# Attention with an interleaved feed-forward part: key projection ahead of the output products in steps 34 to 61

## The reference

```python
x = x + xattn(layernorm(x), ctx, mask, ...)   # 32 heads of 128, 8 batches of 128 tokens
x = x + ffn(layernorm(x), w_gate, w_up, w_down)

def xattn(h, c, mask, position_bias, ln_weight, w_q, w_k, w_v, w_out):
    x = rmsnorm(h, ln_weight)
    q, k, v = x @ w_q.T, c @ w_k.T, c @ w_v.T          # 512 -> 32 * 128
    score = softmax(where(mask, q @ k.T + position_bias, -inf))
    return h + (score @ v) @ w_out.T

def ffn(x, w_gate, w_up, w_down):                       # 512 -> 1376 -> 512
    h = silu(fq(x) @ fq(w_gate).T) * (fq(x) @ fq(w_up).T)
    return fq(h) @ fq(w_down).T                         # fq: 8 bit fake quantization
```

## Time and profile before

| | us |
|---|---|
| median of 3 runs | 1030.38 (1029.58 to 1031.2) |
| the profiled execution, whole | 1029.58 |
| its span, first to last instruction | 1027.9 |
| PE busy | 1005.1 (98%) |
| DVE busy | 690.2 (67%) |
| ACT busy | 512.8 (50%) |
| GpSimd busy | 457.2 (44%) |

### The profile page before, as it was taken

One profiled execution on the slowest core, in us unless ns is written; L12 is line 12 of the kernel. 1 busy time (PEld: TensorE's weight loads), 2 busy tenths in 40 slices (PEclk: granted clock), 3 DMA queues, 4 the chain that ended last, 5 costly groups with the idle time before them and its releaser, 6 DMA issues.

```text
span 1027.9 us, 18615 instructions
## 1 busy us (share of the span) xinstructions
PE 1005.1 (98%) x6215; PEld 848.8 (83%) x6215; DVE 690.2 (67%) x1833; ACT 512.8 (50%) x1298; POOL 457.2 (44%) x361
## 2 busy tenths in 40 slices
PE   8999999999999999999999999999999999998987
PEld 7888888888888888888888888888888888864465
DVE  6666565656658776868765566558656665768977
ACT  4445444444454454444554355254535635546764
POOL 4554444444443454542444435344443634523441
PEclk9999999999999999999999999999999999999999
DMA  7332233332222333332422123222221222100002
GB/s 266 120 100 90 88 99 99 100 100 81 86 90 89 99 101 102 88 122 95 143 88 88 58 65 88 87 68 75 88 64 58 88 88 77 48 21 23 1 1 83
DMA packets 50414, 87.74 MB, mean 85 GB/s; under 512 B 6368, under 2 KB 15200, under 8 KB 50336
## 3 DMA queue, kind: packets, MB, share of 16 engines
q1 hardware_dynamic: 50336, 86.76, 27.2%
HBM read 84.64 MB, written 2.10 MB: 84 GB/s over the span
## 4 chain that ended last, share of the span: by engine, by line
PE 87%; DVE 7%; DVEq 2%; issue 1%; ACT 1%; DMA 0%; POOL 0%; SPq 0%; ACTq 0%
PE pX L1836 17%; PE pX L1838 16%; PE pX L1837 16%; PE pT L2112 6%; PE oacc L1891 5%; PE pS L2036 5%; PE oacc L1898 5%; PE oacc L1895 5%; PE pS L1841 3%; PE pX L1969 1%; PE pT L2025 1%; PE pX L2025 1%; PE pX L1841 1%; DVE silu L1572 1%; DVE h_s L1575 1%
## 5 line engine op out<-in xcount | busy, mean ns | idle before, releaser
L582 POOL TENSOR_TENSOR wq_lo<-raw_q,wq_hi 128x512 fp32r<-128x512 f32 x64 | 82.7, 1292 | 298.2 <-DVE prob L1448 288.5
L1836 PE MATMUL pX<-wv_lo,cT_hi 128*128 128x256 f32 x512 | 149.2, 291 | 0.2 <-ACT q_sb L769 0.2
L897 ACT ACTIVATE prob<-score,neg_max 128x128 f32<-128x128 f32 x256 | 99.8, 391 | 98.3 <-DVE neg_max L1434 98.3
L1837 PE MATMUL pX<-wv_hi,cT_lo 128*128 128x256 f32 x512 | 144.0, 281 | 0.0
L1838 PE MATMUL pX<-wv_hi,cT_hi 128*128 128x256 f32 x512 | 144.0, 281 | 0.0
L582 POOL TENSOR_TENSOR wv_lo<-raw_v,wv_hi 128x1024 fp32r<-128x1024 f32 x32 | 77.1, 2408 | 115.3 <-ACT wv_hi L769 115.3
L1431 DVE TENSOR_TENSOR score<-pS,b_mask 128x512 f32<-128x512 f32 x64 | 44.2, 690 | 121.8 <-PE pS L2036 121.6
L769 ACT ACTIVATE v_sb<-pX 128x512 f32<-128x512 f32 x64 | 38.2, 597 | 160.1 <-PE pX L1838 160.1
L1836 PE MATMUL pX<-xT_lo,wq_hi 128*128 128x512 f32 x252 | 104.4, 414 | 0.7 <-ACT v_sb L769 0.7
L1836 PE MATMUL pX<-cT_lo,wk_hi 128*128 128x512 f32 x252 | 102.4, 406 | 0.0
L1898 PE MATMUL oacc<-wo_hi,aT_lo 128*128 128x512 f32 x256 | 99.9, 390 | 0.2 <-DVE aT_lo L1414 0.2
(11 more groups left out here) (350 smaller groups left out, 2406.2 us busy)
## 6 DMA issues: line engine op xcount, KB each, us to landing
raw_k<-in_wk SPq DMA_DIRECT2D x64, 256.0 KB, 2.8
raw_q<-in_wq SPq DMA_DIRECT2D x64, 256.0 KB, 3.8
raw_v<-in_wv SPq DMA_DIRECT2D x32, 512.0 KB, 3.9
raw_o<-in_wo SPq DMA_DIRECT2D x64, 256.0 KB, 2.7
b_raw<-in_bias SPq DMA_DIRECT2D x64, 64.0 KB, 2.9
g_raw<-in_w_gate SPq DMA_DIRECT2D x16, 172.0 KB
g_raw<-in_w_up SPq DMA_DIRECT2D x16, 172.0 KB
f_raw<-in_w_down SPq DMA_DIRECT2D x4, 688.0 KB, 4.0
```

What stands on the lines that cost most here:

```text
L582: g.tensor_tensor(w_lo[c][:], w_raw[c][:], w_hi[c][:].bitcast(F32), ALU.subtract).then_inc(s_w_lo[c], 1)
L897: e = a.activation(prob[:, b, :], score[:, b, :], ACT.Exp, bias=neg_max[:, b:b + 1], accum_out=row_sum[:, b:b + 1])
L1836: mm(dst, lh, rl, start=start, stop=False, skip_group_check=lint)
L1837: mm(dst, ll, rh, start=False, stop=False, skip_group_check=lint)
```

## The change

One condition. In steps 34 to 61 (before: in step 33 alone, which keeps it) PE's queue has `key_bank_free(n - 1)` and `keys(n + 1)` directly behind `queries(n + 1)`, and the output products and all slices of point 4 behind them. Steps 32, 62 and 63 and the whole first half stay as they are. No other engine's queue is changed.

```diff
@@ -2049,7 +2049,7 @@
 
                     pe.wait_ge(s_v, n + 2 if not isinstance(n, int) else min(n + 2, STEPS))
                     queries(n + 1, next_half)
-                keys_first = isinstance(n, int) and n == H + 1
+                keys_first = isinstance(n, int) and H < n < STEPS - 2
                 if keys_first:
                     key_bank_free(n - 1)
                     keys(n + 1, next_half)
```

## The result

The changed kernel takes 1036.58 us (median of 5 runs, 1035.09 to 1038.92) against 1030.82 of the kernel before in the same comparison: ratio **1.0056**, 95% interval 1.0044 to 1.0068, so +5.8 us (4.5 to 7.0). The forecast was 1037.2, +6.8.

A forecast was written before the change was run, and what follows sets the result against it. PE's own queue was taken as the bound (busy 88.89 of 89.36 us). Key-bank waits of 4.6 plus value-bank waits of 2.2 gave +6.8 us on 1030.38, so 1037.2 us, range 1033.1 to 1040.2.

The forecast's parts named there:

- (1): Twelve gate-chunk steps: PE's keys wait for DVE to empty pX1 of the gate slice; 4.6 us in all.
- (2): Steps 44, 50, 56: value projection waits for DVE to evict the down product from pX0; 0.74 us each, 2.2 in all.
- (3): Up chunks and w_down scales on pT: DVE's eviction still fits before the attention products; 0, at most 0.2 us each.
- (4): Weights and queues moved past: wk_lo, needed 3.4 us earlier, has 5 us cover, and SyncE loads ahead; nothing.
- (5): Step 49: the 0.52 us wait for aT_lo goes, but late prob swallows the gain; 0, bound -0.5 us.
- the swap itself: Keys changing places with outputs and slice on PE: costs nothing, as step 33's 5.44 us for both blocks shows.
- Covered after all: Rival: DVE finishes in time and the value bank returns within the transposes, so no waits; 1029.9 us, chance 2%.
- Collisions of DVE with GpSimd: Rival: later wo_lo meets later DVE tails, so the gate wait grows; +2 to +4 us more, 1040.2 us, chance 10%.
- The clock: Rival: small waits lower PE's granted clock once in each token tile; 6 us more, 1043 us, chance 3%.

The follow-up runs named there:

- the extra reduction: Changed kernel with one more DVE reduction (0.69 us) ahead of each of the twelve gate evictions: 1047.44 us, ratio 1.0166; repeated, 1046.19 us, ratio 1.0155.

## Why the prediction was right, point by point

**The bound.** PE in its own order was the bound, and every lost 0.1 us on it arrived in the total: the step table adds up to the trace's +6.18, and the median has +5.8.

**(1) The wait for the key bank**, forecast 0.44 (512 columns) and 0.28 (352): the steps grew by 0.40 to 0.44, and by 0.23 to 0.25, in step 41 0.33, together 4.4 where 4.6 was written. But a step's growth is not the price of the wait alone. The run with DVE's sooner eviction has the same order on PE and no such wait; against it the outputs start 0.44 later in step 39 (6.81 instead of 6.37 into the step) and 0.28 later in step 53 (6.65 instead of 6.37), and the twelve steps together are 4.68 longer. So this term was right to 0.1 us: a miss of 0.24 (569.89 - 569.65) plus 0.20. The surcharge, 0.19 as taken from the one wait of that kind that the trace had the earlier trace rows, is made of 0.05 from DVE's end to PE's start, 0.11 more to the second product, and 0.04 spread over the other eleven. With a miss four times as long (1.03, the extra reduction) the outputs start at 7.59, 1.22 later than without a wait: again 0.19. Moving DVE's side removed the wait, which shows the cause.

**(2) The wait for the value bank**, forecast 0.74 each, measured 0.63, 0.67, 0.64: 1.94 where 2.2 was written. The term was mis-sized in its restart part. The eviction ended where it was put, 12.64 us into the step (648.08 - 635.44 as predicted, 650.95 - 638.31 as measured). The transposes came 0.06 earlier in the step than before (11.68 instead of 11.74), which makes the miss 0.61 instead of 0.55, and the values started 0.10 behind DVE. But the value projection's first product is slow even without a wait (0.21 to the second in step 44 before, 0.19 with the wait, where 0.12 is the rule), so that part of the restart was already in the old step: the surcharge was 0.08, not 0.19. 0.69 for the wait less the 0.06 of the order gives the 0.63.

**(3) Slices on pT.** "I take 0 and allow 0.2 in each" for steps 37 and 41: measured +0.18, and in step 41 0.08 more than its like. In step 41 of the changed kernel pT_sb ends at 609.28 + 0.68 = 609.96, and the attention products start at 610.03:

```profile
606.91 0.58 DVE L1346 SCALAR_TENSOR_TENSOR e_up<-pT,y_steps,u_row 128x352 f32<-128x352 f32 x1 [4.64 <-PE pT L2025]
...
609.28 0.68 DVE L1478 COPY pT_sb<-pS 128x512 f32<-128x512 f32 x1
...
610.03 1.14 PE L2112 MATMUL pT<-pT_sb,v_sb 128*128 128x128 f32 x8
```

A margin of "about nothing" was a small wait. The 0.08 is there without the wait for the key bank too: with DVE's sooner eviction step 41 is the only gate step longer than before, by 0.05 where its like are 0.03 shorter.

**(4) Weights and queues**: nothing, as written; no wait for wk_lo appears.

**(5) Step 49**: +0.03 for the predicted 0. The wait for aT_lo is gone and the one for prob has taken its place, 0.78 us instead of 0.23 (step 49 before, then changed):

```profile
720.19 0.66 PE L1841 MATMUL pS<-ident,prob 128*128 128x128 f32 x4 [0.23 <-DVE prob L1448]
...
724.76 0.66 PE L1841 MATMUL pS<-ident,prob 128*128 128x128 f32 x4 [0.78 <-DVE prob L1448]
```

**Not seen at all**: the swap itself is not neutral but gains a little, 0.34 us in steps 34 to 36 and 38 and 0.30 in the twelve gate steps (by the run with the sooner eviction). I had claimed that it costs nothing, neither way. A projection takes longer directly behind a slice than behind another projection. Step 34, before and changed:

```profile
500.10 0.48 PE L1836 MATMUL pX<-cT_lo,wk_hi 128*128 128x512 f32 x1
...
502.95 0.60 PE L1841 MATMUL pS<-ident,prob 128*128 128x128 f32 x4
...
498.82 0.39 PE L1836 MATMUL pX<-cT_lo,wk_hi 128*128 128x512 f32 x1
...
501.55 1.07 PE L1891 MATMUL oacc<-wo_hi,aT_hi 128*128 128x512 f32 x4
```

The keys take 2.85 behind the transposes of the slice and 2.73 behind the queries; the transposes of prob, which now stand behind the slice, lose only 0.03 of that. Why a projection loses there, no run shows. It was to be seen in the trace of before (the earlier trace rows has the new order), but I compared only blocks of 5.44 us, not what stands around the slice.

**The rivals.** "Covered after all": no, the misses were on the side where the rows had them. Collisions of DVE with GpSimd: the pair L1470 takes 0.73 us in step 40 and 2.31 in step 48, so it did move, but in none of the twelve gate steps did DVE's score sum start late (1.16 to 1.17 us into the step in each). What runs beside the pair in step 48 is GpSimd's b_mask and wo_lo, one sum and one subtraction, not two subtractions. The clock: full from 490 to 930 us in the changed kernel.

Sum: 6.8 written, 6.2 in the trace. The waits for the key bank came out as written (4.7 for 4.6). The total is lower by 0.3 in (2) and by 0.6 that the order gives back, and higher by 0.2 in step 37, which the sum had at nothing. So the mechanism and its main term were right, and the closeness of the total is partly that small errors of both signs went into it.

## What to carry to other kernels

When a block is moved ahead inside the queue of the engine that is the bound, list the waits that it takes along, and for each subtract the time at which the block will now ask from the end of the other engine's work: what is above zero is the miss. Here a miss counted at its full length plus 0.1 to 0.2 us (0.08 at the value bank, 0.19 to 0.20 at the key bank, down to a miss of 0.08), as often as the step repeats; cover of 3 us becomes none without any row of the old profile showing a wait. The cheaper repair can then lie on the engine that has time: here one DVE operation exchanged with its neighbour gave back what twelve waits of PE had cost, and one pick round moved out of DVE's way in each of two steps was worth more than the whole reordering of PE (2.25 us against 0.6).

## What the runs showed of the hardware that I had not expected

- The price of a PE wait on DVE had parts that stayed the same for misses of 0.24 and 1.03 us: 0.05 us from the end of the DVE record to PE's first product, 0.34 instead of 0.23 to the second, and 0.03 to 0.04 over the rest of the block.
- One idle moment of PE of 2.03 us was followed by eight products at 1.2 GHz (some 1.6 us lost); eleven of 1.51 to 1.71 us in the same run, twelve of up to 0.93 with one extra reduction, and the 1.27 of step 33 were not. One of 1.63 us near the end of the kernel before was followed by a low clock.
- The key projection behind the bf16 transposes of a slice took 0.12 us longer than behind the query projection (2.85 against 2.73 in step 34).
- The same pair of DVE operations on SBUF (L1470) took from 0.49 us with GpSimd idle (step 44 of the changed kernel) to 2.32 with GpSimd's b_mask and wo_lo beside it (step 60 of the changed kernel).
